# A decoder of four layers on one core: gated-delta layer in a new order within a wave, cumulated gates spread over partitions by a DMA, layer norms' roots taken on token rows

## The chip, the cores and the metric

The kernel runs on one core of a Trainium2 chip. A core has a matrix engine (TensorE, PE in the rows, with its weight loads as PEld), three engines for elementwise work (VectorE or DVE, ScalarE or ACT, GpSimd or POOL) and a queue that issues transfers (SyncE, SPq in the rows). Each engine takes its instructions strictly in program order, and engines wait for each other on semaphores. The metric is device time in microseconds of one execution, the median of several runs.

## The reference, cut to what matters

The reference is four transformer layers on x of shape (2, 512, 256): layer norm, attention of some kind, layer norm or none, feed-forward of some kind. What the change touches is the layer norm ahead of each of the four attention layers, and the fourth attention, the gated-delta rule with 16 key heads, 32 value heads and head size 128:

```
def _layernorm(x, axis=-1, eps=1e-05):
    m = jnp.mean(x, axis=axis, keepdims=True)
    v = jnp.var(x, axis=axis, keepdims=True)
    return (x - m) / jnp.sqrt(v + eps)
...
            g_cum = jnp.cumsum(gc, axis=-1)
            g_diff = g_cum[..., :, None] - g_cum[..., None, :]
            decay = jnp.exp(jnp.tril(g_diff))
...
            attn = solve_triangular(eye - L, jnp.broadcast_to(eye, L.shape), lower=True)
...
                v_new = v_i - jnp.matmul(kcd_i, state, precision=prec)
                out_i = jnp.matmul(q_i * jnp.exp(g_i)[..., None], state, precision=prec) + jnp.matmul(a_i, v_new, precision=prec)
                g_last = g_i[..., -1]
                new_state = state * jnp.exp(g_last)[..., None, None] + jnp.matmul(jnp.swapaxes(k_i * jnp.exp(g_last[..., None] - g_i)[..., None], -1, -2), v_new, precision=prec)
```

## The kernel before

The whole decoder is one program. x stays in the core's memory, with its 256 features on two blocks of 128 partitions and the 1024 tokens in the free dimension. Everything is float32.

**layer_norm** (line 56) runs four times. PE averages x over partitions with a matrix of 1/256 (L73), DVE subtracts (L90), ACT squares (L108), PE averages the squares into a full 128x512 tile per half of the tokens (L79), ACT takes its root (L113), DVE its reciprocal (L94, 128x512 elements that are alike on all partitions), and DVE multiplies (L99).

**delta_attention** works in 64 waves: a wave w is one of 16 key heads (h = w // 4) and one of 4 chunks of 128 tokens (c = w % 4), with 4 pairs r of batch and value head at once. Iteration w of the main loop holds pieces of several waves, so that chains of small steps lie beside each other:

- of wave w+2, the preparation: PE spreads the cumulated gates over partitions (L1458, in `make`), by a product of the gates with a triangular matrix, into PSUM bank BG. DVE forms differences (`make_low`, L1871), ACT exponentiates them (`make`: decay L1689, grown L1692), PE forms the key and query scores (L1468, L1470), DVE scales them (`make_scores`, L1879: a_at, a_rough) and makes the matrix to be inverted, v0 (L1888). The sync queue stores v0 and loads its 16x16 diagonal blocks (`spread`, L1348, L1354, L1362), and GpSimd inverts these by substitution in 28 small steps (`substitute`, L1823, L1828, L1832, L1835). `turn_values` and `turn_keys` are transposes (L1477, L1483), `make_qg` is L1893;
- of wave w+1, `gather` (L1371, eight stores, then L1377) brings the small inverses into a_t_narrow;
- of wave w, the rest of the inversion: `widen` on DVE (L1901), then on PE join_a (L1494), close_a (L1506, L1510), join_b (L1519), close_b (L1529, L1531), join_c (L1539), close_c (L1548), each followed by a small copy on DVE or ACT (`close_wa` L1909, `copy_za` L1915, `copy_tb`, `copy_wb`, `copy_half`, `copy_z_half` L1920, `copy_wc`), and `copy_whole`;
- of wave w-1, the recurrence: recall (L1557), `make_right` (L1926), solve (L1565), `new_values` (L1727), answer (L1575, L1576, and the state's growth L1582), `gated` (L1936), `carry` (L1946), `square`, `reduce` (a_var, L1953, L1955), and `root` on GpSimd (a_rstd, L1813);
- of wave w-2, the output: `normed` (L1959), turn_out (L1591), `copy_out` (L1740), project_out (L1602), `add_out` (L1967).

Between them lie the parts (`part(w, n)`) of the projections of coming heads: three of L1418 where c is 2 or 3, two where c is 0, four of the gate projection L1428 where c is 1. Each is copied by ACT (L1666, L1670) and convolved by DVE (`conv(w, j)`, four steps of 128x1024 a wave, L1854 and L1857), then goes through ACT's silu (L1676). From wave 58 on no parts are left.

The order on each engine is written out by hand in the loops at the end of its block. PSUM banks tie it further: parts use banks BG and BK in turn, between the reads of the gates and of the scores.

Of the kernel before, what the change touches and what calls it, by code (L numbers as in the profile page):

```python
# [10 lines left out]
F32 = mybir.dt.float32  # L11
# [44 lines left out]
def layer_norm(nc, name, ps, x, xn, mean_of):  # L56


    with Stage(nc, name) as s:
        square = s.buf("square", [P, KC, N])  # L60
        std = s.buf("std", [P, B, T])
        eps = s.buf("eps", [P, 1])
        mean_ready, centred, squared = s.sem("mean_ready"), s.sem("centred"), s.sem("squared")
        var_ready, std_ready, rstd_ready, normed = (
            s.sem("var_ready"), s.sem("std_ready"), s.sem("rstd_ready"), s.sem("normed"))
        eps_ready = s.sem("eps_ready")
        with nc.Block() as block:

            @block.tensor
            def _(pe):  # L70
# [5 lines left out]
                for b in range(B):  # L76
                    pe.wait_ge(squared, KC * (b + 1))
                    for k in range(KC):
                        mm = pe.matmul(ps[:, B + b, :], mean_of[:, :], square[:, k, b * T:(b + 1) * T],  # L79
                                       start=k == 0, stop=k == KC - 1)  # L80
                    mm.then_inc(var_ready, 1)

            @block.vector
            def _(dve):
# [7 lines left out]
                for b in range(B):  # L92
                    dve.wait_ge(std_ready, b + 1)
                    dve.reciprocal(std[:, b, :], std[:, b, :]).then_inc(rstd_ready, 1)  # L94
                    dve.wait_ge(rstd_ready, b + 1)
                    dve.wait_ge(squared, KC * (b + 1))
                    for k in range(KC):
                        part = slice(b * T, (b + 1) * T)
                        dve.tensor_tensor(xn[:, k, part], xn[:, k, part], std[:, b, :],  # L99
# [3 lines left out]
            def _(act):  # L103
# [7 lines left out]
                for b in range(B):  # L111
                    act.wait_ge(var_ready, b + 1)
                    act.activation(std[:, b, :], ps[:, B + b, :], ACT.Sqrt,  # L113
                                   bias=eps[:, 0:1]).then_inc(std_ready, 1)
# [1102 lines left out]
def delta_attention(nc, ps, d, x, xn):  # L1217
# [15 lines left out]
    t_dram = nc.dram_tensor("a3_t_dram", (2, P, 2, PR, SB), F32).ap()  # L1233
    with Stage(nc, "a3") as s:
# [7 lines left out]
        half = s.buf("half", [P, PR])  # L1242
        gates = s.buf("gates", [P, KINDS * TT, VH])
# [18 lines left out]
        def sems(*names):  # L1262
# [9 lines left out]
        (gc_ready, kq_ready, vrow_psum, krow_psum, low_ready, decay_ready, grown_ready) = sems(  # L1272
            "gc_ready", "kq_ready", "vrow_psum", "krow_psum", "low_ready", "decay_ready", "grown_ready")
# [8 lines left out]
        (ks_psum, rest_ready, x_psum, vnew_ready, o_psum, ds_psum, state_ready) = sems(  # L1282
            "ks_psum", "rest_ready", "x_psum", "vnew_ready", "o_psum", "ds_psum", "state_ready")
# [60 lines left out]

# [871 lines left out]
```

## Time and profile before

| | us |
|---|---|
| median of 3 runs | 2885.48 (2884.47 to 2887.69) |
| the profiled execution, device time | 2888.33 |
| its span, first to last instruction | 2886.6 |
| PE busy | 2389.7 (83%) |
| DVE busy | 1545.3 (54%) |
| POOL busy | 985.5 (34%) |
| ACT busy | 931.0 (32%) |
| delta_attention's waves, from the first `widen` to the last | 1338.72 to 2777.71 |

Half of the span is the 64 waves. PE is the busiest engine, so the question in each stretch is what PE waits for, and at which clock it runs. The granted clock is given as a share of full speed: 1.00 is 2.4 GHz and 0.50 is 1.2 GHz. Durations of matmuls are modelled, so the distance between two starts is the safer measure; where the text says "start to start", it is that. A row such as "x4" merges four instructions.

### The profile page before, as it was taken

The numbers are of one execution on the slowest core, as the hardware profiler recorded it, in microseconds if no ns is written. First come the engines' busy times: TensorE is split into PE (matmuls) and PEld (weight loads), VectorE is DVE, ScalarE is ACT, GpSimd is POOL, SyncE is SP. The second block draws the span as 40 slices with busy tenths as digits, with TensorE's granted clock in tenths as the row PEclk, the third lists the DMA queues.
The fourth block names the chain that finished last, engine by engine and source line by source line (L and its number), as shares of the span: only waits on it lengthen the run. The fifth ranks groups of instructions, "written<-read, shape, count | busy, mean of one in ns | idle before, by whom it ended". The sixth has DMA issues, their size and how long they took to land. (4 is left out here: it accounts for less than half of the span.)

```text
span 2886.6 us, 48059 instructions
## 1 busy us (share of the span) xinstructions
PE 2389.7 (83%) x18052; PEld 1459.9 (51%) x18052; DVE 1545.3 (54%) x2863; ACT 931.0 (32%) x1896; POOL 985.5 (34%) x2123
## 2 busy tenths in 40 slices
PE   6597999986897958747888888888888888888879
PEld 3234444433332425334566656666666666666753
DVE  1632555657753142335666666666666666666531
ACT  1162111101152122123444434444444434443421
POOL 1310001110002001305555555555555555555520
PEclk8798999998798989967999999999999999999989
DMA  1002010101001000011111111111111111111100
GB/s 48 1 0 76 22 37 28 44 0 35 1 1 45 0 28 17 16 31 34 23 36 34 35 27 27 35 37 27 28 35 36 27 34 27 35 38 21 26 13 15
DMA packets 183490, 78.06 MB, mean 27 GB/s; under 512 B 133200, under 2 KB 164464, under 8 KB 183152
## 3 DMA queue, kind: packets, MB, share of 16 engines
q1 hardware_dynamic: 183280, 75.23, 10.0%
q8 instruction: 136, 2.23, 0.3%
q14 instruction: 74, 0.61, 0.1%
HBM read 52.10 MB, written 22.02 MB: 26 GB/s over the span
## 5 line engine op out<-in xcount | busy, mean ns | idle before, releaser
L1832 POOL TENSOR_TENSOR a_z<-a_z,a_term 32x14 f32<-32x14 f32 (+6 forms) x896 | 342.8, 383 | 70.2
L1828 POOL TENSOR_TENSOR a_term<-a_z,a_l 32x14 f32<-32x14 f32 (+6 forms) x896 | 333.6, 372 | 70.2
L1418 PE MATMUL ps<-all_xn,a_w_qkv 128*128 128x512 f32 x512 | 311.4, 743 | 6.2 <-ACT a_grown L1692 4.1
L1005 POOL TENSOR_TENSOR all_x<-all_x,f_part_out 128x512 f32<-128x512 f32 x64 | 85.0, 1365 | 634.3 <-DVE f_part_out L977 634.3
L878 PE MATMUL ps<-all_xn,f_w 128*128 128x512 f32 x640 | 287.8, 594 | 1.9 <-ACT f_share L896 1.9
L1857 DVE SCALAR_TENSOR_TENSOR a_qkv<-a_raw,a_taps,a_qkv 128x1024 f32<-128x1024 f32 x192 | 245.2, 1277 | 2.5
L1823 POOL TENSOR_TENSOR a_z<-a_l,a_ident 32x256 f32<-32x256 f32 x64 | 47.0, 735 | 563.7 <-DMA a_l<-a_v_dram 563.7
L878 PEld LDWEIGHTS ps<-all_xn,f_w 128*128 128x128 f32 x640 | 122.2, 191 | 155.8 <-issue 155.8
L1666 ACT ACTIVATE a_raw<-ps 128x512 f32<-128x512 f32 x128 | 76.5, 597 | 365.8 <-PE ps L1418 365.8
L1494 PE MATMUL ps<-a_t_wide,a_v_off 32*32 32x32 f32 x2048 | 33.9, 211 | 179.9 <-DVE a_t_wide L1901 179.9
L864 PE MATMUL ps<-f_gated,f_w 128*128 128x512 f32 x320 | 155.1, 612 | 20.9 <-DVE f_part_out L977 20.9
L985 DVE TENSOR_TENSOR f_gated<-f_act_h,ps 128x512 f32<-128x512 f32 x80 | 55.0, 688 | 215.0 <-ACT f_act_h L901 214.8
L901 ACT ACTIVATE f_act_h<-ps 128x512 f32<-128x512 f32 x80 | 47.8, 597 | 375.8 <-PE ps L878 375.8
L1428 PE MATMUL ps<-a_w_z,all_xn 128*128 128x256 f32 x512 | 153.3, 453 | 16.8 <-ACT a_zs L1670 16.8
L1602 PE MATMUL ps<-a_out_t,a_w_out 128*128 128x256 f32 x512 | 133.4, 405 | 40.3 <-ACT a_out_t L1740 26.3
L1418 PEld LDWEIGHTS ps<-all_xn,a_w_qkv 128*128 128x128 f32 x512 | 104.1, 223 | 97.2 <-issue 92.0
L1936 DVE SCALAR_TENSOR_TENSOR a_xf<-ps,a_zs 128x512 f32<-128x512 f32 x64 | 44.2, 691 | 190.2 <-PE ps L1576 190.2
L1915 DVE COPY a_za<-ps 32x128 f32<-32x128 f32 x128 | 37.1, 290 | 182.8 <-PE ps L1510 181.9
L1494 PEld LDWEIGHTS ps<-a_t_wide,a_v_off 32*32 32x32 f32 x2048 | 26.1, 122 | 205.6 <-DVE a_t_wide L1901 205.6
L1428 PEld LDWEIGHTS ps<-a_w_z,all_xn 128*128 128x128 f32 x512 | 110.3, 226 | 36.0 <-ACT a_zs L1670 17.2
L1602 PEld LDWEIGHTS ps<-a_out_t,a_w_out 128*128 128x128 f32 x512 | 95.7, 197 | 59.2 <-ACT a_out_t L1740 31.1
L864 PEld LDWEIGHTS ps<-f_gated,f_w 128*128 128x128 f32 x320 | 61.6, 195 | 102.9 <-issue 72.8
(261 smaller groups left out, 4903.3 us busy)
## 6 DMA issues: line engine op xcount, KB each, us to landing
a_v_dram<-a_v SPq DMA_DIRECT2D x64, 256.0 KB, 2.0
f_w<-in_f_w SPq DMA_DIRECT2D x24, 512.0 KB, 4.9
a_w_qkv<-in_a_w SPq DMA_DIRECT2D x16, 512.0 KB, 3.8
a_t_dram<-a_z SPq DMA_DIRECT2D x512, 8.0 KB
a_w_z<-in_a_w SPq DMA_DIRECT2D x16, 256.0 KB, 2.8
a_w_out<-in_a_wo SPq DMA_DIRECT2D x16, 256.0 KB, 2.8
a_v_off<-a_v SPq DMA_DIRECT2D x256, 4.0 KB, 1.8
a_l<-a_v_dram SPq DMA_DIRECT2D x256, 8.0 KB
```

The lines of the kernel that those rows point to most:

```text
L864: mm = pe.matmul(ps[:, 4 + b * KC + m, :], w2[:, v, f, m * P:(m + 1) * P], gated[:, (v * TILES + i) % 4, :], start=f == 0, stop=f == FT - 1)
L878: mm = pe.matmul(ps[:, bank + n % 2, :], w[:, v, k, f * P:(f + 1) * P], xn[:, k, b * T:(b + 1) * T], start=k == 0, stop=k == KC - 1)
L985: dve.tensor_tensor(gated[:, n % 4, :], act_h[:, n % 2, :], ps[:, 2 + n % 2, :], ALU.mult).then_inc(gated_ready, 1)
L1005: pool.tensor_tensor(part, part, part_out[:, n, :], ALU.add).then_inc(added, 1)
L1418: mm = pe.matmul(ps[:, to, :], w_qkv[:, k, mt * P:(mt + 1) * P], xn[:, k, b * T:(b + 1) * T], start=k == 0, stop=k == KC - 1)
L1428: mm = pe.matmul(ps[:, to, i * 256:(i + 1) * 256], xn[:, k, tt * P:(tt + 1) * P], w_z[:, k, :], start=k == 0, stop=k == KC - 1)
L1494: mm = pe.matmul(narrow(BW)[q, r, :], v0_off[q, w % 3, r, :], t_wide[q, 1, r, :], start=True, stop=True)
L1602: mm = pe.matmul(bank(BO)[:, B * m:B * (m + 1), :], w_out[:, v, m * P:(m + 1) * P], out_t[:, v::VPK, :], start=v == 0, stop=v == VPK - 1)
L1666: act.activation(raw[:, mt, b, TAPS - 1:], ps[:, of, :], ACT.Copy).then_inc(raw_ready, 1)
L1828: pool.tensor_tensor(term[:, 0:j, j + 1:], z[:, 0:j, j:j + 1].broadcast_to([HP, j, n]), rows[:, j:j + 1, j + 1:].broadcast_to([HP, j, n]), ...
L1832: pool.tensor_tensor(z[:, 0:j, j + 1:], z[:, 0:j, j + 1:], term[:, 0:j, j + 1:], ALU.add).then_inc(sub_step, 1)
L1857: dve.scalar_tensor_tensor(to, rows, tap, to, ALU.mult, ALU.add).then_inc(conv_ready if j == TAPS - 1 else conv_step, 1)
```

## The change

**Gates.** Before the waves, two products turn the cumulated gates so that tokens lie in the free dimension (a_g_turned), ACT copies them, and a DMA stores them to a_g_dram. In each iteration the sync queue loads those of wave w+3, spread over all 128 partitions by the transfer, into a_g_row (`load_gates`, 256 KB). `make_low` and ACT's `grow` read a_g_row instead of bank BG. The four products L1458 of each wave are gone.

**Order.** PE begins an iteration with recall, scores and the first part; the half of answer that needs only the state is a step of its own (`ask`), ahead of solve; join_a stands after the second part; the state's growth comes ahead of the answer; turn_out ahead of close_b; project_out ahead of the last part. DVE takes normed ahead of the scores, v0 ahead of `widen`, carry ahead of `gated`, and `make_qg` last. ACT and GpSimd are ordered anew too: on GpSimd `root(w-1)` stands ahead of `substitute(w+2)`.

**Layer norm.** The averages of the squares are taken with tokens on partitions, one column for 128 tokens, so that root and reciprocal work on 128x4 elements; products with a broadcast column and the identity (eight of 128x128 in each norm, 32 in all) spread them again, and DVE multiplies from PSUM. The identity is one more transfer at the program's start.

```
-                    dve.reciprocal(std[:, b, :], std[:, b, :]).then_inc(rstd_ready, 1)
-                    dve.wait_ge(rstd_ready, b + 1)
+                    dve.reciprocal(rstd[:, of], rstd[:, of]).then_inc(rstd_ready, 1)
+                for b in range(B):
+                    dve.wait_ge(spread, b + 1)
...
+                def load_gates(w):
+
+                    if w >= 2:
+                        sp.wait_ge(low_ready, PR * (w - 1))
+                        sp.wait_ge(grown_ready, w - 1)
+                    c, h = w % CH, w // CH
+                    row = g_dram.rearrange("(b c) (h v) t -> c h b (v t)", b=B, v=VPK)[c, h]
+                    sp.dma_start(g_row[:, w % 2, :, :].rearrange("p (b v) t -> p b (v t)", b=B),
+                                 row.partition_broadcast(P)).then_inc((g_even, g_odd)[w % 2], 16)
...
-                    for r in range(PR):
-                        mm = pe.matmul(bank(BG)[:, r, :], gate(K_G, w, r).to_broadcast([P, P]), upto[:, :],
-                                       start=True, stop=True)
-                    mm.then_inc(gc_ready, 1)
...
                 for w in range(-2, W + 1):
+                    if made(w - 1):
+                        root(w - 1)
                     if made(w + 2):
                         substitute(w + 2)
-                    if made(w - 1):
-                        root(w - 1)
...
                         dve.scalar_tensor_tensor(low[:, r, :], bank(BG)[:, r, :], gate(K_GC, w, r), floor[:, :],
-                        dve.scalar_tensor_tensor(low[:, r, :], g_row[:, w % 2, r, :], gate(K_GC, w, r), floor[:, :],
```

On PE, in an iteration with three parts, from the first piece of the iteration on. Before:

```order
L1458 MATMUL ps<-a_upto,a_gates 128x128 x4
L1468 MATMUL ps<-a_qkv 128x128 x2
L1470 MATMUL ps<-a_qkv 128x128 x2
L1557 MATMUL ps<-a_state,a_qkv 128x256 x2
L1494 MATMUL ps<-a_t_wide,a_v_off 32x32 x16
L1418 MATMUL ps<-all_xn,a_w_qkv 128x512 x2
L1565 MATMUL ps<-a_rest,a_inv 128x128 x4
L1477 MATMUL ps<-a_ident,a_qkv 128x128 x4
L1506 MATMUL ps<-a_t_wide,a_wa 32x32 x16
```

After, on PE at the same place (L1587 is recall, L1496 and L1498 the scores, L1452 a part, L1604 ask, L1595 solve, L1507 turn_values, L1524 join_a, L1621 the state's growth, L1536 and L1540 close_a):

```order
L1587 MATMUL ps<-a_state,a_qkv 128x256 x2
L1496 MATMUL ps<-a_qkv 128x128 x2
L1498 MATMUL ps<-a_qkv 128x128 x2
L1452 MATMUL ps<-all_xn,a_w_qkv 128x512 x2
L1604 MATMUL ps<-a_state,a_qg 128x128 x4
L1595 MATMUL ps<-a_rest,a_inv 128x128 x4
L1507 MATMUL ps<-a_ident,a_qkv 128x128 x4
L1452 MATMUL ps<-all_xn,a_w_qkv 128x512 x2
L1524 MATMUL ps<-a_t_wide,a_v_off 32x32 x16
L1621 MATMUL ps<-a_v_new,a_k_row 128x128 x4
L1536 MATMUL ps<-a_t_wide,a_wa 32x32 x16
L1540 MATMUL ps<-a_wa,a_t_wide 32x32 x12
```

join_a, which takes what `widen` writes, has moved behind two parts, ask, solve and turn_values.

On DVE, from the end of one iteration into the next. Before:

```order
L1967 TENSOR_TENSOR all_x<-all_x,ps 128x4x128
L1871 SCALAR_TENSOR_TENSOR a_low<-ps,a_gates,a_floor 128x128 x4
L1926 SCALAR_TENSOR_TENSOR a_rest<-ps,a_gates,a_v_row 128x128 x4
L1879 TENSOR_TENSOR a_at<-ps,a_decay 128x512
L1879 TENSOR_TENSOR a_rough<-ps,a_decay 128x512
L1901 TENSOR_TENSOR a_t_wide<-a_t_narrow,a_side 128x256
L1888 SCALAR_TENSOR_TENSOR a_v<-a_rough,a_gates,a_strict 128x128 x4
L1959 TENSOR_TENSOR a_xnorm<-a_xf,a_rstd 128x512
```

After, on DVE:

```order
L2025 TENSOR_TENSOR all_x<-all_x,ps 128x4x128
L1950 TENSOR_TENSOR a_qg<-a_qkv,a_grown 128x512
L1925 SCALAR_TENSOR_TENSOR a_low<-a_g_row,a_gates,a_floor 128x128 x4
L1983 SCALAR_TENSOR_TENSOR a_rest<-ps,a_gates,a_v_row 128x128 x4
L2017 TENSOR_TENSOR a_xnorm<-a_xf,a_rstd 128x512
L1931 TENSOR_TENSOR a_rough<-ps,a_decay 128x512
L1931 TENSOR_TENSOR a_at<-ps,a_decay 128x512
L1945 SCALAR_TENSOR_TENSOR a_v<-a_rough,a_gates,a_strict 128x128 x4
L1958 TENSOR_TENSOR a_t_wide<-a_t_narrow,a_side 128x256
```

`widen` (L1901, now L1958) has moved behind v0 and normed, and a_low is made from a_g_row, without a product ahead of it.

## Rows read from the trace of the kernel before

**Rows 1.** The page's line on engines: busy us, share of the span, instructions.

```profile
PE 2389.7 (83%) x18052; PEld 1459.9 (51%) x18052; DVE 1545.3 (54%) x2863; ACT 931.0 (32%) x1896; POOL 985.5 (34%) x2123
```

**Rows 2.** Busy time, clock, DMA: 58 iterations, then one with three, two and four parts.

```profile
core 0: us, PE busy (x) PEld busy (x) DVE busy (x) ACT busy (x) POOL busy (x), PEclk, DMA share, GB/s
1339.20:2688.70 1349.50, 1150.73 (x13180) 871.13 (x13180) 862.96 (x1861) 583.79 (x1301) 762.74 (x1801) 0.92 0.14 32
...
1850.64:1874.22 23.58, 19.91 (x227) 14.28 (x227) 14.95 (x34) 8.41 (x21) 13.36 (x31) 0.93 0.10 20
...
1897.92:1919.14 21.22, 17.59 (x214) 12.63 (x215) 14.21 (x31) 9.50 (x22) 11.48 (x28) 0.91 0.18 48
1919.14:1945.04 25.90, 23.16 (x246) 19.77 (x246) 15.45 (x34) 13.89 (x27) 15.07 (x35) 0.88 0.16 39
```

**Rows 3.** Who waited for whom in the 58 iterations: us in total, times, longest.

```profile
PE ps L1494 <- DVE a_t_wide L1901: 165.8, 58, 8.9
```

**Rows 4.** PE in order of time: start, us, line, count, idle before and its releaser.

```profile
1850.64 0.65 PE L1494 MATMUL ps<-a_t_wide,a_v_off 32*32 32x32 f32 x32 [2.74 <-DVE a_t_wide L1901]
1851.22 3.26 PE L1418 MATMUL ps<-all_xn,a_w_qkv 128*128 128x512 f32 x4
1854.32 1.05 PE L1565 MATMUL ps<-a_rest,a_inv 128*128 128x128 f32 x8
...
1856.40 1.98 PE L1418 MATMUL ps<-all_xn,a_w_qkv 128*128 128x512 f32 x4
...
1866.06 1.97 PE L1602 MATMUL ps<-a_out_t,a_w_out 128*128 128x256 f32 x8 [0.93 <-issue]
...
1868.56 1.16 PE L1458 MATMUL ps<-a_upto,a_gates 128*128 128x128 f32 x8
1869.55 0.61 PE L1468 MATMUL ps<-a_qkv 128*128 128x128 f32 x4
...
1919.72 3.78 PE L1428 MATMUL ps<-a_w_z,all_xn 128*128 128x256 f32 x8
1923.30 1.91 PE L1565 MATMUL ps<-a_rest,a_inv 128*128 128x128 f32 x8
```

**Rows 5.** DVE in order of time, the same iteration's end.

```profile
1869.86 1.12 DVE L1871 SCALAR_TENSOR_TENSOR a_low<-ps,a_gates,a_floor 128x128 f32<-128x128 f32 x4
...
1873.75 0.41 DVE L1901 TENSOR_TENSOR a_t_wide<-a_t_narrow,a_side 128x256 f32<-128x256 f32 x1
```

**Rows 6.** GpSimd's small steps beside DVE: one held, then one that isn't.

```profile
1885.97 1.31 POOL L1828 TENSOR_TENSOR a_term<-a_z,a_l 32x54 f32<-32x54 f32 x1
...
1885.86 1.28 DVE L1857 SCALAR_TENSOR_TENSOR a_qkv<-a_raw,a_taps,a_qkv 128x1024 f32<-128x1024 f32 x1
...
1319.57 1.56 DVE L1888 SCALAR_TENSOR_TENSOR a_v<-a_rough,a_gates,a_strict 128x128 f32<-128x128 f32 x4
1319.60 0.30 POOL L1832 TENSOR_TENSOR a_z<-a_z,a_term 32x54 f32<-32x54 f32 x1
```

**Rows 7.** GpSimd's substitution from first step to root; the gather's issues.

```profile
1857.61 0.71 POOL L1823 TENSOR_TENSOR a_z<-a_l,a_ident 32x256 f32<-32x256 f32 x1 [9.24 <-DMA a_l<-a_v_dram]
...
1872.22 1.01 POOL L1813 TENSOR_TENSOR a_rstd<-a_var,a_half 128x4 f32<-128x4 f32 x1
...
1856.28 5.64 SPq L1371 DMA_DIRECT2D a_t_dram<-a_z  x8
1863.29 0.35 SPq L1377 DMA_DIRECT2D a_t_narrow<-a_t_dram  x1
```

**Rows 8.** The load of a_t_narrow: KB, median us from issue to landing.

```profile
a_t_narrow<-a_t_dram SPq DMA_DIRECT2D x43, 64.0 KB, 1.8
```

**Rows 9.** DVE in order of time, the last `widen`.

```profile
2777.71 0.41 DVE L1901 TENSOR_TENSOR a_t_wide<-a_t_narrow,a_side 128x256 f32<-128x256 f32 x1
```

**Rows 10.** The layer norm ahead of the delta layer, DVE in order of time.

```profile
1220.88 3.35 DVE L94 RECIPROCAL n_std<-n_std 128x512 f32<-128x512 f32 x1 [2.70 <-ACT n_std L113]
...
1228.86 1.29 DVE L99 TENSOR_TENSOR all_xn<-all_xn,n_std 128x512 f32<-128x512 f32 x2
```

## What is predicted for the changed kernel

> **What bounds the kernel now.** The page's line on engines comes first: PE is busy for 83% of the span, nobody else for more than 54% [rows 1]. Then the table of stretches [rows 2]: in 58 iterations of the delta layer, 1349.5 us, PE is busy for 1150.7, DVE for 863, GpSimd for 763. So an iteration takes 1349.5 / 58 = 23.27 us, of which PE works 19.8. Two things in it are not work. The list of waits has the first: join_a waits for `widen` in every iteration, 165.8 / 58 = 2.86 us [rows 3]. The second is the clock: PE is granted 1.00 when dense, and the stretches show a mean of 0.92. In PE's order of time [rows 4], the part right behind the wait takes 3.26 us, the next, equal one 1.98 us; with four parts it is 3.78, and solve behind it 1.91 against 1.05. PE stood idle before, so its clock had fallen from 2.4 to 1.2 GHz.
>
> Why does `widen` come late? Not for its data: from `low` at 1869.86 to `widen` at 1873.75 [rows 5] DVE works through low, rest, at and rough, and low itself had to wait for PE's product L1458 at 1868.56 [rows 4]. It is a queue's order, 1874.2 - 1868.6 = 5.6 us long, of which PE can fill about half.
>
> **The change part by part.** All sums are against the profiled execution (2888.33 us, span 2886.6); it lies 2.8 us over the median, and I take that off at the end.
>
> *PE's own work in an iteration.* From 23.27 us go: the idle time at join_a, 2.86; the products L1458, 1869.55 - 1868.56 = 0.99 start to start; the idle 0.93 ahead of project_out (out_t was copied late; now two steps and, mostly, a part stand between), which the iteration with four parts does not have, so 0.7 on average; and the half clock: 3.26 - 1.98 = 1.28 in three of four iterations and (3.78 - 1.98) + (1.91 - 1.05) = 2.66 in the fourth, 1.63 on average. Left are 23.27 - 6.18 = 17.1 us. That is PE's floor if nothing else ends last.
>
> *Does the new order hide `widen`?* I walked an iteration with three parts. On PE, full clock, in us from its start: recall and scores to 1.9, part to 3.7, ask to 4.6, solve to 5.5, turn_values to 6.1, part to 7.9, join_a to 8.5, growth to 9.4, close_a 10.1, answer 11.0, join_b and turn_keys 11.7, turn_out 12.3, close_b 12.6, part 14.5, join_c 15.1, project_out 17.0, close_c 17.6. DVE's tail waits for project_out: add_out to 17.9, qg 18.6, low 19.7, which is 2.1 in the next iteration; then rest 3.2, normed 3.8, rough 4.4, at 5.0, v0 6.1, `widen` 6.4. PE's second part needs at (5.0 against 6.1), join_a needs `widen` (6.4 against 7.9), solve needs rest (3.2 against 4.6). Each has 1.0 to 1.6 us to spare. DVE's work is 14.9 us an iteration [rows 2] and fits. What is late next: in the iteration with two parts, copy_half stands behind copy_out on ACT, and join_c waits some 1.5 us, 0.4 on average. That makes 17.5.
>
> *The gates' DMA.* It is issued in the iteration before the one that reads it, so its landing is covered; on the sync queue it adds one issue, 0.35 us as L1377 [rows 7]. What is queued behind it is `spread`, which waits for v0 anyway. If it came late, low would, with about 1 us to spare. DVE now reads the gates from SBUF; I keep 1.12 us for the four [rows 5].
>
> *GpSimd's chain.* This is the new risk. `root(w-1)` now stands ahead of `substitute(w+2)` and waits for the variance, which is ready some 1.3 us before PE's iteration w ends. From there: root 1.0; substitution S; stores 1863.29 - 1856.28 = 7.0; load 1.8 [rows 7, 8]; `widen` 0.4; semaphores some 0.8; together S + 11.0. It must end by join_a in iteration w+2, so in 1.3 + P + 7.9 for a period P: P >= S + 1.8. Its own load asks for P >= S + 1.1. Today S is 1872.22 - 1857.61 = 14.6 [rows 7]. Some steps are held by DVE's convolutions: 1.31 us instead of 0.3, beside a DVE instruction of 1.28 [rows 6]; three of them are in that S, so 11.5 is the floor. The ceiling: today GpSimd is idle while DVE makes v0, normed and `widen`; now it is not. With v0 (1.1), normed (0.6) and low (1.1) each holding it, S is 17.5 and P 19.3. But beside v0 GpSimd's steps stay at 0.30 and DVE gives way: v0's four instructions take 1.56, where low's like four take 1.12 [rows 5, 6]. I take S = 16, nearer to 14.6: P >= 17.8.
>
> On this the Trainium skill, page "SBUF — State Buffer", section "SBUF: two separate sides", says that a DVE instruction with two SBUF inputs and a GpSimd instruction exclude each other, and whichever starts first keeps the shared ports to its end. By that rule, `low`, which used to read PSUM and now reads a_g_row and floor, joins the convolutions as a holder, against this change. The rows of v0 and of the convolution agree with either side losing; the rule alone would put S up by at most low's 1.1 us.
>
> So P lies between 17.1 (PE) and 19.3 (GpSimd's ceiling); I take 18.2, since several floors (17.5, 17.8) lie close together and meet with jitter. 58 x (23.27 - 18.2) = **294 us**.
>
> *The last five iterations* have no parts: (2777.71 - 2688.7) / 5 = 17.8 us each [rows 2, 9]. There PE is no bound and S loses its convolutions; with S near 12 and the shorter iteration I estimate 15.4: **12 us**. Bounds 0 and 18.
>
> *Layer norms.* From the first reciprocal at 1220.88 to the end at 1228.86 + 1.29 = 1230.15 are 9.3 us [rows 10]. Now: two reciprocals of 128x4, at most 0.28 each, as one quarter of low's 1.12 [rows 5]; products for one half, 0.5; semaphores 0.3; four multiplications, 2.6. That is 4.0, saving 5.3 in each of four: **21 us**, between 16 and 24 (PSUM reads may cost a little, the root on 4 columns is shorter). The averages of squares are 8 small products for each half in place of 4 wide ones; by L1458's 0.25 each 2.0 us, as before.
>
> *Added once:* two products, a copy, a store and a load ahead of the waves, beside DVE's 16 convolution steps for head 0; and one transfer at the start, 0.5 to 1 us. **Cost 1 us.**
>
> Sum: 294 + 12 + 21 - 1 = 326. 2888.3 - 326 - 2.8 = 2559.5, so **2560 us**.
>
> **The rivals.**
> *GpSimd's chain ends last.* DVE's denser queue holds more steps, S = 17.5, P = 19.3: 58 x 3.97 = 230, with the rest 262, so 2623. For it: all slack on this chain is 0.4 us at S = 16. Against it: DVE gives way beside v0. Then join_a would wait again, for a DMA, not for DVE.
> *The clock does not come back.* PE waits still (join_c, join_a at times) and keeps the 1.63 us of half clock: P = 19.8, 58 x 3.5 = 201, with the rest 233: 2652. For it: the clock fell behind a wait of only 2.8 us. Against it: gaps of 0.9 us ahead of project_out left L1602 at full clock, 1.97.
> *Slower than before.* The same chain by another size: `substitute` can no longer start when its blocks have landed but only behind the variance, so inverse and recurrence form one loop. It costs 58 us for each us of S over 16.4, and eats all gains where P = 23.27 + 32 / 58 = 23.8, so S = 22, a mean step of 0.75 us instead of 0.5. At S = 23 it gives 58 x 1.5 = 87 more than before less 32, 2941 us. Nothing shows steps that slow over a whole substitution.
> *Nothing comes of it*, because some engine's new order closes a loop that I did not walk: 2880 to 2890.
>
> **How the numbers follow.** Forecast, P from 17.2 to 18.9: 58%; GpSimd's chain, 18.9 to 19.5: 17%; the clock, about 19.8: 13%; both together or worse, still faster, 2670 to 2870: 6%; below 2500: 2%; no change: 1%; slower: 3%. The range from PE's floor (17.1: 2496) to the two rivals is 2505 to 2665. Since 0.2% (6 us) is about what a measurement of this kernel can tell from no change, faster is 0.96, same 0.01, slower 0.03.
>
> **What would show it.** In the table of stretches, an iteration of 18.2 us and a PE clock near 1.00. In the list of waits, join_a behind DVE gone or under 0.3 us; if GpSimd's chain ends last, `widen` waits for the load of a_t_narrow, and GpSimd is busy above 90%. GpSimd's first step should wait for DVE's variance through root, not for a DMA; S is the distance from root to the copy at its end. The norms' end is 4 us behind the first reciprocal. I am wrong if PE still waits 1 us or more an iteration, for whatever.

## The result, and the profile of the kernel after

The changed kernel takes **2563.24 us** (median of 4 runs, 2555.99 to 2569.95), beside 2886.56 us for the kernel before on the same chip: a ratio of 0.888, interval 0.885 to 0.891. The forecast was 2560 us in 2505 to 2665. The profiled execution of after took 2568.62 us with a span of 2566.8, so against the profiled one of before (2888.33) the gain to be explained is 319.7 us. The page's line on engines, as [rows 1]:

```profile
PE 2268.3 (88%) x17704; PEld 1381.7 (54%) x17704; DVE 1553.0 (61%) x2863; ACT 923.1 (36%) x1897; POOL 955.5 (37%) x2123
```

The table of stretches for the 58 iterations from the first `widen`, with the columns of [rows 2]:

```profile
1351.60:2383.30 1031.70, 996.97 (x12727) 769.24 (x12728) 895.89 (x1863) 578.58 (x1303) 727.37 (x1787) 0.99 0.26 56
```

1031.7 / 58 = **17.79 us** an iteration where there were 23.27. PE is busy for 97% of it (996.97 of 1031.7 us), at a granted clock of 0.99 instead of 0.92. Its work shrank too, from 1150.7 to 997.0 us: the same matmuls less L1458, at full clock. PE's list of waits in this stretch (us in total, times, longest), as [rows 3]:

```profile
PE ps L1524 <- DVE a_t_wide L1958: 13.9, 9, 7.1
PE ps L1569 <- ACT a_t_half L1765: 9.6, 15, 0.7
PE ps L1536 <- DVE a_wa L1966: 7.0, 15, 0.5
```

join_a's wait fell from 165.8 us to 13.9, 7.1 of them in one wave. The two lines below it are 0.6 and 0.5 us in one iteration of four, the one with two parts. The three together are 30.5 / 58 = 0.53 us an iteration; by the table PE is without work for 1031.7 - 997.0 = 34.7 us in all. An iteration with three parts, PE in order of time:

```profile
1900.89 1.13 PE L1587 MATMUL ps<-a_state,a_qkv 128*128 128x256 f32 x4
...
1902.75 1.88 PE L1452 MATMUL ps<-all_xn,a_w_qkv 128*128 128x512 f32 x4
...
1906.69 1.88 PE L1452 MATMUL ps<-all_xn,a_w_qkv 128*128 128x512 f32 x4
1908.50 0.45 PE L1524 MATMUL ps<-a_t_wide,a_v_off 32*32 32x32 f32 x32
...
1913.27 1.98 PE L1452 MATMUL ps<-all_xn,a_w_qkv 128*128 128x512 f32 x4
...
1918.31 0.92 PE L1587 MATMUL ps<-a_state,a_qkv 128*128 128x256 f32 x3
```

From recall to recall are 1918.31 - 1900.89 = 17.42 us; the walk in the prediction had 17.6. No row has idle time ahead of it, and all three parts take 1.88 to 1.98, where the one behind the wait had taken 3.26 [rows 4]. DVE in the same iteration, as [rows 5]:

```profile
1901.60 1.69 DVE L1925 SCALAR_TENSOR_TENSOR a_low<-a_g_row,a_gates,a_floor 128x128 f32<-128x128 f32 x4
...
1904.24 0.73 DVE L2017 TENSOR_TENSOR a_xnorm<-a_xf,a_rstd 128x512 f32<-128x512 f32 x1
...
1906.09 1.38 DVE L1945 SCALAR_TENSOR_TENSOR a_v<-a_rough,a_gates,a_strict 128x128 f32<-128x128 f32 x4
1907.40 0.41 DVE L1958 TENSOR_TENSOR a_t_wide<-a_t_narrow,a_side 128x256 f32<-128x256 f32 x1
```

`widen` ends at 1907.8 and join_a starts at 1908.5: even with v0 and normed ahead of it, it is 0.7 us early. The walk had 1.5; DVE lost the difference beside GpSimd: low took 1.69 us where the prediction kept 1.12, v0 1.38. That low's input is the reason shows in order_only below, where low reads PSUM again and takes 1.12 us in the middle of its waves; here it takes 1.68. GpSimd, from one root to the next:

```profile
1900.29 1.01 POOL L1867 TENSOR_TENSOR a_rstd<-a_var,a_half 128x4 f32<-128x4 f32 x1 [5.34 <-DVE a_var L2013]
1901.28 0.99 POOL L1877 TENSOR_TENSOR a_z<-a_l,a_ident 32x256 f32<-32x256 f32 x1
...
1906.25 0.35 POOL L1886 TENSOR_TENSOR a_z<-a_z,a_term 32x54 f32<-32x54 f32 x1
...
1914.25 1.25 POOL L1886 TENSOR_TENSOR a_z<-a_z,a_term 32x14 f32<-32x14 f32 x1
1915.56 0.60 POOL L1889 COPY a_z<-a_z 32x256 f32<-32x256 f32 x1
1916.87 1.01 POOL L1867 TENSOR_TENSOR a_rstd<-a_var,a_half 128x4 f32<-128x4 f32 x1 [0.71 <-DVE a_var L2013]
```

The substitution takes 1916.16 - 1901.28 = 14.9 us here. The first step has no wait of its own behind root, as the prediction said it should be. Over 45 waves, counted the same way, S has a mean of 13.9 (11.8 to 15.1); before it was 14.4.

**Where the time went.** Span against span, from start to start of rows that both traces have (`widen` at 1338.72 before and 1351.15 after is the first):

| stretch | before | after | change |
|---|---|---|---|
| start to the load of a_w_ba (delta layer) | 1231.1 | 1239.2 | +8.1 |
| from there to the first `widen` | 107.6 | 111.9 | +4.3 |
| 58 iterations | 1350.0 | 1031.7 | -318.3 |
| last five iterations | 89.0 | 79.6 | -9.4 |
| from the last `widen` on | 108.9 | 104.4 | -4.5 |

The first line is odd, since all four norms lie in it and each became shorter. In it the attention with ALiBi, from its load of a_wq to the feed-forward's load of f_su_ug, took 230.1 us before and 247.5 after, and the change touches none of it but one norm's place beside it. The rows are in the part on the prediction's steps.

### The profile page after: what moved, and what is told of

It reads as the page before. It is cut to its first block and busy times, and to the rows that moved or that the text cites. A ratio compares the mean times of both kernels' runs of the same rounds, so it can differ in the third digit from the quotient of the medians.

```text
span 2566.8 us, 47706 instructions
## 1 busy us (share of the span) xinstructions
PE 2268.3 (88%) x17704; PEld 1381.7 (54%) x17704; DVE 1553.0 (61%) x2863; ACT 923.1 (36%) x1897; POOL 955.5 (37%) x2123
## 5 line engine op out<-in xcount | busy, mean ns | idle before, releaser
L1882 POOL TENSOR_TENSOR a_term<-a_z,a_l 32x14 f32<-32x14 f32 (+6 forms) x896 | 319.3, 356 | 70.2
L1886 POOL TENSOR_TENSOR a_z<-a_z,a_term 32x14 f32<-32x14 f32 (+6 forms) x896 | 315.2, 352 | 70.2
L1452 PE MATMUL ps<-all_xn,a_w_qkv 128*128 128x512 f32 x512 | 249.8, 613 | 9.9 <-DVE a_at L1931 9.9
L1462 PE MATMUL ps<-a_w_z,all_xn 128*128 128x256 f32 x512 | 129.2, 398 | 18.0 <-ACT a_zs L1718 16.5
L1867 POOL TENSOR_TENSOR a_rstd<-a_var,a_half 128x4 f32<-128x4 f32 x64 | 65.0, 1016 | 209.8 <-DVE a_var L2013 157.2
L1452 PEld LDWEIGHTS ps<-all_xn,a_w_qkv 128*128 128x128 f32 x512 | 89.7, 194 | 79.0 <-issue 67.9
L1462 PEld LDWEIGHTS ps<-a_w_z,all_xn 128*128 128x128 f32 x512 | 97.6, 198 | 32.8 <-ACT a_zs L1718 16.9
L1778 ACT ACTIVATE a_v_new<-ps,a_gates 128x128 f32<-128x128 f32 x256 | 72.7, 366 | 111.8 <-PE ps L1595 111.8
L1643 PEld LDWEIGHTS ps<-a_out_t,a_w_out 128*128 128x128 f32 x512 | 94.7, 195 | 17.4 <-ACT a_out_t L1791 2.2
L1925 DVE SCALAR_TENSOR_TENSOR a_low<-a_g_row,a_gates,a_floor 128x128 f32<-128x128 f32 x256 | 96.1, 433 | 6.7 <-DMA a_g_row<-a_g_dram 6.7
L280 ACT ACTIVATE a_probs<-ps 128x512 f32<-128x512 f32 x128 | 65.8, 607 | 80.0 <-PE ps L245 79.8
```

Source lines behind the costliest of these rows:

```text
L1452: mm = pe.matmul(ps[:, to, :], w_qkv[:, k, mt * P:(mt + 1) * P], xn[:, k, b * T:(b + 1) * T], start=k == 0, stop=k == KC - 1)
L1462: mm = pe.matmul(ps[:, to, i * 256:(i + 1) * 256], xn[:, k, tt * P:(tt + 1) * P], w_z[:, k, :], start=k == 0, stop=k == KC - 1)
L1643: mm = pe.matmul(bank(BO)[:, B * m:B * (m + 1), :], w_out[:, v, m * P:(m + 1) * P], out_t[:, v::VPK, :], start=v == 0, stop=v == VPK - 1)
L1778: act.activation(v_new[:, r, :], bank(BR)[:, r, :], ACT.Copy, scale=gate(K_BETA, w, r)).then_inc(vnew_ready, 1)
L1882: pool.tensor_tensor(term[:, 0:j, j + 1:], z[:, 0:j, j:j + 1].broadcast_to([HP, j, n]), rows[:, j:j + 1, j + 1:].broadcast_to([HP, j, n]), ...
L1886: pool.tensor_tensor(z[:, 0:j, j + 1:], z[:, 0:j, j + 1:], term[:, 0:j, j + 1:], ALU.add).then_inc(sub_step, 1)
```

## The experiments

**order_only**: the new order and the new norms, but the gates by products again. `make_gates(w+2)` opens PE's iteration; low and grown read its bank.

```diff
                 for w in range(-2, W + 2):
+                    if made(w + 2):
+                        make_gates(w + 2)
                     if made(w - 1):
...
-                        dve.scalar_tensor_tensor(low[:, r, :], g_row[:, w % 2, r, :], gate(K_GC, w, r), floor[:, :],
+                        dve.scalar_tensor_tensor(low[:, r, :], bank(BG)[:, r, :], gate(K_GC, w, r), floor[:, :],
```

> The changed kernel with its new order and norms, but the cumulated gates made again by four products on PE at the start of each iteration (0.99 us start to start), read from PSUM by low and grown; no gates' DMA. My theory (PE's own work is the floor, and each product or wait on PE adds in full): 0.99 us for the products and 0.9 us because the first part must wait until ACT has read the bank, so 17.8 + 1.9 = 19.7 us an iteration, 64 x 1.9 = 120 us more than the changed kernel, less 6 us for the load's wait ahead of the waves: about 2677. Rival (the order alone carries the gain, the products hide in slack): within 15 us of 2563. Rival (the DMA carries it): above 2800.

Measured: 2651.0 us, ratio 0.918 (0.916 to 0.919); both rivals fall, and the theory was 26 us too slow. Iterations of 1119.5 / 58 = 19.30 us, 1.51 more than after, where it had 1.9. PE's waits in them:

```profile
PE ps L1444 <- ACT a_grown L1743: 19.6, 28, 0.7
PE ps L1444 <- issue: 9.2, 14, 0.7
PE ps L1527 <- DVE a_t_wide L1955: 4.7, 1, 4.7
```

So the order alone already hides `widen` (4.7 us in 58 iterations). What the DMA adds is the products' 0.99 us and the wait of the first part for grown, which must be read out of the bank before the part may write it: (19.6 + 9.2) / 58 = 0.50, where I had expected 0.9. Order and norms carry 2886 - 2651 = 235 us, the DMA the last 88.

**gates_only**: the kernel before with the DMA in place of the products, nothing else.

```diff
-                    for r in range(PR):
-                        mm = pe.matmul(bank(BG)[:, r, :], gate(K_G, w, r).to_broadcast([P, P]), upto[:, :],
-                                       start=True, stop=True)
...
+                    if made(w + 3):
+                        load_gates(w + 3)
```

> The kernel before with the gates' DMA alone: old order, old norms, four products fewer on PE in each iteration. My theory: join_a still waits for widen, since low, rest, at and rough stand ahead of it on DVE, and rest waits for recall; only 0.9 us an iteration goes, 23.3 to 22.4, 58 us in all, 2830; PE's wait at join_a stays at 2.5 to 3 us and the part behind it stays at half clock. Rival (the product ahead of low was what made widen late): the wait shrinks to about 1 us and the clock comes back, 20 us an iteration, about 2680.

Measured: 2847.9 us, ratio 0.985 (0.983 to 0.988). Iterations of 1303.4 / 58 = 22.47 us, 0.8 less than before. join_a's wait in them:

```profile
PE ps L1506 <- DVE a_t_wide L1921: 191.7, 58, 13.4
```

It is 3.3 us an iteration, larger than the 2.86 it was [rows 3]: PE comes to join_a earlier and DVE's queue is as long as ever. The iteration is as expected, and the theory was 18 us too fast for the whole; half of the miss lies in the last five iterations (18.55 us each, before 17.8) and in the layer's start (5 us more). The DMA is worth 38 us in the old order and 88 in the new one.

**join_late**: the kernel before with join_a behind part, solve and turn_values, on PE alone.

```diff
-                    if made(w):
-                        join_a(w)
                     part(w, 0)
...
                     if made(w):
+                        join_a(w)
                         close_a(w)
```

> The kernel before with a single step of PE moved: join_a behind the first part, solve and turn_values. My theory (the wait and the half clock hang on this one place): the wait of 2.86 us and 1.63 us of half clock go, close_a now waits some 0.9 us for DVE's close_wa, which stands behind v0 and normed: 23.3 to 20.0 us an iteration, about 2700 in all. Rival (only the whole order does it; the wait moves to another step): less than half of that, above 2790.

Measured: 2808.1 us, ratio 0.974 (0.971 to 0.976), iterations of 21.83 us; the rival had it right, the theory was 108 us too fast. PE's waits, then DVE's:

```profile
PE ps L1506 <- DVE a_wa L1908: 84.6, 58, 3.4
...
PE ps L1418 <- ACT a_grown L1691: 21.6, 28, 0.9
...
PE ps L1494 <- DVE a_t_wide L1900: 4.7, 1, 4.7
```

```profile
DVE a_xnorm L1958 <- POOL a_rstd L1812: 62.1, 29, 3.4
```

join_a's own wait is gone, 4.7 us in all. It stands one step on, at close_a: DVE makes wa behind v0 and normed, and normed waits in 29 waves for a root that stands on GpSimd behind a whole substitution. The wait at close_a is 84.6 / 58 = 1.46 us. Part of it is no queue: close_a now stands right behind join_a, and in few_parts below, where the two also stand side by side, the way to DVE and back alone costs 0.45. So moving the waiting instruction moved some 1.0 us of the wait to the next one that hears from the same queue. The change moves normed, v0 and root with it; of these only root's place was tested by itself, in the next run.

**root_last**: after, with one swap on GpSimd, `root(w-1)` behind `substitute(w+2)` as it was.

```diff
-                    if made(w - 1):
-                        root(w - 1)
                     if made(w + 2):
                         substitute(w + 2)
+                    if made(w - 1):
+                        root(w - 1)
```

> The changed kernel with one swap undone: on GpSimd root(w-1) stands behind substitute(w+2) again. My theory (root had to move, since normed now stands ahead of the scores on DVE): normed(w-1) waits for root, which waits for the substitution, which waits for the blocks of v0, which DVE makes behind normed: a loop of spread and load 6.1, substitution 14.5, root 1.0, normed 0.6, rough and at 1.2, v0 1.3, semaphores 0.4, together 25 us an iteration, slower than before the change: about 2990. Rival (the place of a 1 us step on an engine that idles 2.9 us an iteration is neutral): 2563.

Measured: 2874.9 us, ratio 0.997 (0.994 to 1.000), iterations of 23.15 us: one swap takes back all but 11 us of the 323. I had expected it slower still, by 115 us; S is 12.95 here and not the 14.5 put into the loop. The loop itself shows in its rows, GpSimd first, then DVE:

```profile
1904.94 1.01 POOL L1867 TENSOR_TENSOR a_rstd<-a_var,a_half 128x4 f32<-128x4 f32 x1
1914.84 0.71 POOL L1877 TENSOR_TENSOR a_z<-a_l,a_ident 32x256 f32<-32x256 f32 x1 [8.89 <-DMA a_l<-a_v_dram]
...
1928.06 1.01 POOL L1867 TENSOR_TENSOR a_rstd<-a_var,a_half 128x4 f32<-128x4 f32 x1
```

```profile
1905.99 0.69 DVE L2017 TENSOR_TENSOR a_xnorm<-a_xf,a_rstd 128x512 f32<-128x512 f32 x1 [5.93 <-POOL a_rstd L1867]
1907.79 1.13 DVE L1945 SCALAR_TENSOR_TENSOR a_v<-a_rough,a_gates,a_strict 128x128 f32<-128x128 f32 x4
```

root, normed, v0, the blocks' way through DRAM (1908.9 to 1914.8, and GpSimd idle for 8.89 us), the substitution, root again: 1928.06 - 1904.94 = 23.1 us, the iteration's length. Since DVE's normed now stands ahead of v0, root must stand ahead of the substitution. The two places are one decision.

**slow4 and slow9**: after, with 4 and with 9 spare copies of 32x256 on GpSimd ahead of each substitution, to find what the substitution's length costs.

```diff
+                    for n in range(9):
+                        if spare_count[0]:
+                            pool.wait_ge(spared, spare_count[0])
+                        pool.tensor_copy(spare[:, :], ident16[:, :]).then_inc(spared, 1)
+                        spare_count[0] += 1
```

> The changed kernel with four more copies of 32x256 ahead of each substitution on GpSimd, writing to a buffer that nobody reads: S grows by some 2.8 us, from about 14.2 to 17.0. My theory, P >= S + 1.8 us: 18.8 us an iteration instead of 17.8, 58 us more, 2621. Rival (GpSimd's idle time of 2.9 us an iteration is free slack): no change, 2563.

> The same with nine copies: S about 20.5. My theory: P = 22.3, 58 x 4.5 = 260 us more, 2823; between this and slow4 each us of S costs 58 us. Rival (the chain has 2.9 us of slack, then GpSimd's own load counts): 58 x 3.4 = 197 more, 2760.

Measured: 2603.6 us (0.902, 0.899 to 0.904) and 2703.3 us (0.936, 0.933 to 0.939). The copies were cheaper than expected: four took 1.89 us. The row of slow9's nine, and its waits of `widen` and of join_a:

```profile
1904.02 4.36 POOL L1881 COPY a_spare<-a_ident 32x256 f32<-32x256 f32 x9
```

```profile
DVE a_t_wide L1964 <- DMA a_t_narrow<-a_t_dram: 131.1, 48, 11.3
```

```profile
PE ps L1525 <- DVE a_t_wide L1964: 102.9, 41, 10.9
```

With the copies counted in, the three kernels stand so (S by the mean over 45 waves):

| | S | S + 1.8 | iteration |
|---|---|---|---|
| after | 13.9 | 15.7 | 17.79 |
| slow4 | 14.4 + 1.9 = 16.3 | 18.1 | 18.72 |
| slow9 | 14.3 + 4.4 = 18.7 | 20.5 | 20.11 |

At S = 18.7 the prediction's rule, P >= S + 1.8, comes within 0.4 us, and the wait has the form it named: join_a behind `widen`, `widen` behind the load of a_t_narrow. At 16.3 the iteration lies 0.6 over what either bound asks: join_a waits for `widen` in 23 of the 58 iterations, 42.6 us in all, so GpSimd's chain ends last in some waves and PE in the others. After itself stands on PE's side. Both whole times came out below what I had expected, 2621 and 2823 us, because the copies were cheaper, and for slow4 above the rival's 2563: GpSimd's idle time is not free slack.

**old_norms**: after with the layer norm of before.

```diff
-                dve.reciprocal(rstd[:, of], rstd[:, of]).then_inc(rstd_ready, 1)
...
+                    dve.reciprocal(std[:, b, :], std[:, b, :]).then_inc(rstd_ready, 1)
```

> The changed kernel with the four layer norms as before. By the rows after the change a norm lasts 17.6 us against 20.2 to 20.6, so I expect 11 us more, 2574; the prediction's 5.3 us for each norm would give 21 more, 2584. The waves should not move.

Measured: 2573.2 us, ratio 0.891 (0.889 to 0.893). Its median is 10 us over after's, as expected, but the traces show that this is no measure of the norms. The norms are 14 us longer than in after, the attention with ALiBi is 17.4 us shorter (230.1), and the 58 iterations, which should not have moved, are 16.7 us longer (18.08 us each, clock 0.98). The two medians also come from different chips, and single runs of after spread over 14 us, so the last pair of runs measures it again.

**gates_early**: after, with the store of the gates and the first load ahead of the sync queue's wait for z, as the table above points there.

```diff
-                sp.wait_ge(z_ready, 4)
-                load_z(1)
                 sp.wait_ge(turned, 1)
...
                 load_gates(0)
+                sp.wait_ge(z_ready, 4)
+                load_z(1)
```

> The changed kernel with the store of the cumulated gates and the first load moved ahead of the wait for the gate projection on the sync queue. In the changed kernel's trace they are issued 25 us after the gates are ready, and the first low waits 6.7 us for the load. My theory: this wait goes, 5 to 7 us less, 2557 in the median. Rival (the start is bound by DVE's convolutions and by what follows low anyway): no change.

**after_again**: after, unchanged, on the same chip.

> The changed kernel itself, beside the two above on the same chip: 2563, with single runs near 2556 and near 2569. If the two levels come from the stretch of half clock in the second layer's attention, whose code the change did not touch, a trace of a run near 2556 shows that stage some 13 us shorter.

Measured: 2545.7 us (0.881, 0.879 to 0.883) against 2552.0 us (0.886, 0.883 to 0.889). From the load of a_w_ba to the first `widen` it is 104.1 us, in after_again 112.4. The store's issue and low in gates_early:

```profile
1272.26 0.37 SPq L1421 DMA_DIRECT2D a_g_dram<-a_g_turned  x1
...
1298.41 1.05 DVE L1925 SCALAR_TENSOR_TENSOR a_low<-a_g_row,a_gates,a_floor 128x128 f32<-128x128 f32 x4
```

The copy of a_g_turned starts at 1271.87, the store goes out at its end, and low waits for no DMA. The gain in that stretch, 8.3 us, is a little more than the 5 to 7 expected, and the whole time moved by 6.3.

**few_parts**: gates_early, with copy_half ahead of copy_out, and wa ahead of the first convolution, in iterations with two parts, to take the two small waits out of PE's list.

```diff
+                    if made(w) and few:
+                        copy_half(w)
                     if made(w - 2):
                         copy_out(w - 2)
...
-                    if not late:
+                    if not late and w % CH:
                         conv(w, 0)
```

> gates_early, and two swaps in the iterations with fewer than three parts: ACT copies half ahead of out, and DVE (where no state grows) takes close_wa ahead of the first convolution step. PE's waits there are 9.6 us for half and 7.0 us for wa in 58 iterations of the changed kernel. My theory: PE is the floor, so both come off in full, 12 to 16 us less than gates_early, 2543. Rival (project_out then waits for out, and the convolution's delay comes back later in DVE's queue): within 4 us of gates_early.

Measured: 2557.1 us (0.887, 0.885 to 0.890), no gain over gates_early and by the medians 11 us slower; its iterations take 17.88 us, those of gates_early 17.82, which is 4 us of that; the rest is not explained. PE's waits:

```profile
PE ps L1569 <- ACT a_t_half L1765: 7.2, 15, 0.5
PE ps L1536 <- DVE a_wa L1969: 6.8, 15, 0.5
PE ps L1643 <- DVE a_xf L1996: 6.3, 13, 0.7
```

The theory fell, both waits are still there and a third came. With two parts nothing stands on PE between join_a and close_a, so its wait for wa is the way to DVE and back, not a place in a queue.

**early_again and early_old_norms**: gates_early, unchanged, and gates_early with the layer norm of before, on one chip. They ask what the norms are worth, and whether the long ALiBi attention (the first line of the table) comes with them.

> gates_early, unchanged, beside the next kernel on one chip. Of eight profiled executions with the new layer norms four had the ALiBi attention (load of a_wq to load of f_su_ug) at 229 to 233 us and four at 247; of four with the old norms all were at 227 to 230. Theory A (the level goes with the run, whatever the norms): single runs of both kernels lie in two groups some 15 us apart. Theory B (the new norms make the long level possible): only this kernel shows two groups, about 2530 and 2546 us. Median 2546 expected by the run before.

> gates_early with the layer norm of before. The new norms save 2.7 us each by the rows, 11 in all. Theory A (the long ALiBi attention has nothing to do with the norms): the median is 11 us over early_again's, about 2557, and single runs spread over some 15 us in two groups as early_again's do. Theory B (the long one comes with the new norms alone): single runs lie within 8 us of each other, the stage is at 227 to 233 us, and the median is 2540 to 2551, within 5 us of early_again's, since the norms' 11 us are given back there in part of the runs.

Measured: 2556.5 us (2544.4 to 2578.6; ratio 0.887, 0.884 to 0.889) and 2579.1 us (2561.0 to 2584.1; 0.892, 0.890 to 0.894). The new norms save 0.0057 of 2890 us, 16 us, give or take 10. In the profiled executions the spans are 16.5 us apart and the load of a_w_ba 12.3, issued at 1218.5 and 1230.8. In that, the four norms themselves are 16.8 us shorter, and the stages between them 4.5 longer, the ALiBi attention 2.4 of it. Another 8.6 us lie in the iterations, 18.03 us with the old norms and 17.88 with the new. old_norms had shown the same, 18.08, while after, after_again and gates_early lie at 17.78 to 17.82. No step of the edit stands there, and why they differ is open, so the 16 us can't be put down to the norms alone. Theory B falls: with the old norms single runs spread over 23 us, with the new ones over 34. Theory A's two groups are not there either, the runs lie all over their range; and the profiled execution with the old norms again had the ALiBi attention at 230.0 us. The level of gates_early differs between chips too (0.881 there, 0.887 here), so that the whole run doesn't tell it from after; the stretch it changes is 104.2 us again.

## Why the prediction was right, and where its parts were not

**What bounds the kernel, and that the new order hides it: right.** join_a's 2.86 us are gone to 0.24, without GpSimd or a DMA taking the place, and the clock came back: 0.99 in the stretch, full length for every part. order_only shows that the order does this without the DMA. join_late and root_last show that parts of the order don't do it: join_a's move alone gives 78 us, and the whole order without root's move 11. The other moves (ask, growth, turn_out, project_out, ACT's order) were not taken back one by one, so which of them the gain needs is not shown.

**The iteration: 17.79 measured, 18.2 taken, 24 us too cautious over 58.** The term mis-sized is S. I took 16 with a ceiling of 17.5, expecting DVE's v0, normed and low to hold GpSimd's steps; it was 13.9, less than before. In the rows above GpSimd's step beside v0 takes 0.35 and DVE's four instructions stretch to 1.38. Beside DVE's other work fewer steps were held to their full length: those over 1.0 us went from 3.0 in a wave to 1.8, those of 0.45 to 1.0 from 1.2 to 3.1. A smaller term is join_c's wait for copy_half: forecast at 1.5 us in one iteration of four, 0.4 on average, it was 0.64 and 0.17, while close_a's wait for wa, 0.12 on average, was not in the sum. So P went not by S + 1.8 but by PE: 17.42 in the iteration walked, 0.53 on average for the waits left. The walk and the floor of 17.1 bracket it: 17.79 - 0.53 = 17.26. That the chain was near was right: S + 2.4 us costs 0.9 an iteration, S + 4.8 costs 2.3.

The Trainium skill, page "SBUF — State Buffer", section "SBUF: two separate sides", was cited for low becoming a holder of the shared ports, at most 1.1 us on S. Where low reads PSUM, in order_only, S is 13.15, in after 13.87: 0.7, within it. But in the old order the same edit moves S only from 14.4 to 14.5 (gates_only), so the runs don't pin it. Beside GpSimd's first step both lost: low took 1.69 for 1.12, the step 0.99 where root_last's took 0.71. That low itself would pay was no term of the sum; it took most of the 0.8 us by which `widen` came nearer to join_a than walked.

**The last five iterations: 9.4 saved, 12 forecast.** Right within its bounds.

**The norms: 13 us saved in this execution, 21 forecast; one norm as forecast, three about half.** From the first reciprocal to the end they took 6.7, 4.1, 6.5 and 6.7 us, each 9.3 before. The norm ahead of the delta layer, as [rows 10]:

```profile
1227.79 1.84 PE L83 MATMUL ps<-all_mean_of,n_square 128*128 128x1 f32 x16
...
1229.99 3.26 PE L83 MATMUL ps<-all_mean_of,n_square 128*128 128x1 f32 x16 [0.36 <-ACT n_square L121]
...
1231.55 0.18 DVE L106 RECIPROCAL n_rstd<-n_rstd 128x4 f32<-128x4 f32 x1 [2.27 <-ACT n_rstd L127]
1233.12 3.76 PE L90 MATMUL ps<-all_ident,n_rstd 128*128 128x128 f32 x16
...
1236.92 1.28 DVE L112 TENSOR_TENSOR all_xn<-all_xn,ps 128x512 f32<-128x512 f32 x2 [0.42 <-PE ps L90]
```

From the first reciprocal to the end are 1238.20 - 1231.55 = 6.65 us, where I had 4.0. I priced the small products by L1458's 0.25 us, taken at full clock. The granted clock of these two stretches:

```profile
1229.99:1233.25 3.26, 3.26 (x17) 3.26 (x17) 0.18 (x1) 1.51 (x2) 0.00 (x0) 0.56 0.02 5
1233.12:1236.88 3.76, 3.76 (x17) 3.46 (x17) 1.46 (x3) 0.26 (x1) 0.00 (x0) 0.50 0.00 0
```

PE ran the spread at its lower level, 1.2 GHz, after it had worked in short pieces with idle time between them. The same 16 records of averages take 1.84 at full clock and 3.26 at 0.56; the spread's eight products took 3.76, where 0.25 each makes 2.0. The reciprocal went better than said, 0.18 for 3.35. The second norm, ahead of the ALiBi attention, met the other clock: its averages ran at 1.00, its spread at a mean of 0.78.

```profile
655.27 0.18 DVE L106 RECIPROCAL n_rstd<-n_rstd 128x4 f32<-128x4 f32 x1 [2.31 <-ACT n_rstd L127]
655.50 2.51 PE L90 MATMUL ps<-all_ident,n_rstd 128*128 128x128 f32 x16
...
656.70 2.63 DVE L112 TENSOR_TENSOR all_xn<-all_xn,ps 128x512 f32<-128x512 f32 x4 [0.56 <-PE ps L90]
```

Here the end is 656.70 + 2.63 - 655.27 = 4.06 us behind the first reciprocal, the 4.0 of the forecast, though with luck in its terms: I had 0.56 for two reciprocals, of which 0.18 stands in the way, and 0.5 for the four products of one half, which at 0.25 each are 1.0. So the term that failed is the clock. It differs by place and by run. In the nine profiled executions with the new norms the same stretch took 3.9 to 4.3 us in the second norm and 6.6 to 6.7 in the fourth; the first took 3.9 to 4.9 in four of them, the third 4.6 to 4.7 in five, and both 6.3 to 6.8 in the others. I made for the norms the mistake that I had charged to the old order in the waves, a duration without its clock.

**Added once: 1 us forecast, 4.3 measured.** The extra transfer at the program's start costs next to nothing: the first norm starts at 6.63 us instead of 6.50, where I had 0.5 to 1. I priced the store and load, and not the place of the store in the sync queue. The rows of after:

```profile
1281.11 0.36 ACT L1813 ACTIVATE a_g_turned<-ps 128x256 f32<-128x256 f32 x1
1306.27 0.47 SPq L1423 DMA_DIRECT2D a_g_dram<-a_g_turned  x1
1309.20 1.36 SPq L1369 DMA_DIRECT2D a_g_row<-a_g_dram  x2
1314.40 1.14 DVE L1925 SCALAR_TENSOR_TENSOR a_low<-a_g_row,a_gates,a_floor 128x128 f32<-128x128 f32 x4 [6.73 <-DMA a_g_row<-a_g_dram]
```

The data were there at 1281.5, the store went out at 1306.3, behind a wait for z, and DVE then stood 6.73 us. gates_early takes this away, and 8.3 us of the stretch with it, twice what the change had added.

**What nobody touched: +21 us.** The stretch between the third norm and the fourth is 3.8 us longer, the attention with ALiBi 17.4. Twenty us of the ALiBi attention, of after and then of before:

```profile
784.50:804.50 20.00, 20.00 (x64) 5.19 (x63) 3.46 (x8) 6.12 (x9) 0.00 (x0) 0.50 0.00 0
804.50:824.50 20.00, 20.00 (x83) 5.81 (x84) 7.65 (x14) 7.31 (x11) 1.27 (x1) 0.76 0.00 1
```

```profile
791.50:811.50 20.00, 20.00 (x112) 6.17 (x112) 9.28 (x18) 10.67 (x16) 1.27 (x1) 1.00 0.00 1
```

PE is busy without a gap in all of them, and in after it is granted 0.50 where before it is granted 1.00; it does 64 matmuls in the time of 112. Ahead of them it had had idle time in both, 15.63 of 20 us busy in after and 16.18 before. The same code as after, in after_again, has the attention in 232.5 us, and its profiled execution has a span 20 us shorter, 2546.9. Of nine profiled executions with the new norms four had it at 247 and five at 229 to 232; the five with the old norms had it at 227 to 230. In the four with the long attention the third norm, a feed-forward later, took 15.5 us from its first DVE instruction to its last, in the five others 12.2. So it goes with the run, and more than one stage goes with it; whether the new norms, which shift what comes ahead of it, make the long one likelier, fourteen executions don't tell. Together this eats most of the 13 to 19 us that the norms save by their own rows: the load of a_w_ba comes at 1226 us on average over the nine and at 1231 over the five. Why the clock stays down in one run and rises in another through the same code is open.

**The sum** was 326 us and the gain 319.7, closer than its terms: the iterations gave 24 more than forecast, the end 4.5 that I had not counted, the norms 8 less, the start 3 less, the last five iterations 3 less, and the untouched stages took 21. That these nearly cancel is luck. The two rivals of 2623 and 2652 us did not come, but both are real: slow9 has the first's wait, and the half clock sits in the norms.

## What to carry to other kernels

When a wait is an engine's queue order and not its data, walk the queues of all engines around it: moving only the waiting instruction moves the wait to the next instruction that hears from the same queue, and one step left in its old place can close a loop as long as the old iteration. Price small instructions at the clock they will meet: behind idle time it was the lower one in three norms of four, so a range has to hold both. Look for what a stage is worth in its own rows and not in the whole time alone, which here moved by 14 us and more between runs of one kernel. Look at where a new DMA stands in its queue, at the program's start too: the wait ahead of it there cost more than the transfer.

## What the runs showed that I had not expected

- PE busy without a gap for 20 us (x64 matmuls) at a granted clock of 0.50, and with the same code in another run at 1.00: 232 or 247 us for one stage.
- DVE's small instructions with both inputs in SBUF stretch beside GpSimd's small steps: four of 128x128 took 1.69 and 1.38 us instead of 1.12, and S fell from 14.4 to 13.9 although GpSimd works beside more of them. The same four with one input in PSUM took 1.12 (order_only).
- Layer norms of one program, alike but for the data, met different granted clocks: 4.1 us in one place and 6.5 to 6.7 in three others of the same execution.
- A copy of 32x256 on GpSimd, four or nine in a row, each waiting for the last, takes 0.48 us (4.36 / 9).
